# VectorE turns the normalized y of all chunks, and B with x, in a fused Mamba-2 and LoRA layer

## What is computed

```python
x = x + attn(xn) + ffn(xn)                     # xn = layernorm(x), [1, 2048, 1024]
# attn, a Mamba-2 mixer: 64 heads of 64, 8 groups, state size 128
proj = xn @ in_proj_w.T                        # gate 4096 | x 4096, B 1024, C 1024 | dt 64
xBC  = silu(causal_conv4(proj[x|B|C]) + conv_bias)
dt   = softplus(dt + dt_bias);  dA = exp(-dt * exp(A_log))
state = state * dA_t + (dt_t * x_t) B_t        # scan over the tokens, per head
y_t  = state C_t + D * x_t
yn   = y * rsqrt(mean(y*y over the group's 512) + eps) * norm_w * silu(gate)
attn = yn @ out_proj_w.T
# ffn: xn @ W_base.T + b_base, plus the top-2 of 8 rank-16 LoRA experts
```

## Time and profile before

| | |
|---|---|
| median of 3 runs | 3144.74 us (3143.58 to 3145.55) |
| profiled execution, own time | 3145.09 us |
| its span, first to last instruction | 3143.4 us |
| PE, PEld busy | 3126.1 us (99%), 2573.4 us (82%) |
| DVE, ACT, POOL busy | 2558.5 (81%), 1704.5 (54%), 835.5 us (27%) |
| granted clock of TensorE, mean | 1.000 |

### The profile page before, as it was taken

One profiled execution on the slowest core, in us unless ns is written; L12 is line 12 of the kernel. 1 busy time (PEld: TensorE's weight loads), 2 busy tenths in 40 slices (PEclk: granted clock), 3 DMA queues, 4 the chain that ended last, 5 costly groups with the idle time before them and its releaser, 6 DMA issues.

```text
span 3143.4 us, 55218 instructions
## 1 busy us (share of the span) xinstructions
PE 3126.1 (99%) x17660; PEld 2573.4 (82%) x17660; DVE 2558.5 (81%) x4599; ACT 1704.5 (54%) x4467; POOL 835.5 (27%) x917
## 2 busy tenths in 40 slices
PE   8999999999999999999999999999999999999999
PEld 7788888887888888888788888888878888888887
DVE  7977777785589999999648999999954988989983
ACT  5766666664265555656226555556533655565551
POOL 4444434433022222222103222222210222222220
PEclk9999999999999999999999999999999999999999
DMA  8777777777665555555566555555546555555554
GB/s 290 274 265 272 264 276 266 261 256 263 232 216 194 189 201 187 189 194 201 173 225 205 191 191 191 201 184 190 209 166 236 196 195 187 195 194 201 186 189 161
DMA packets 185668, 672.63 MB, mean 214 GB/s; under 512 B 21056, under 2 KB 22208, under 8 KB 185408
## 3 DMA queue, kind: packets, MB, share of 16 engines
q1 hardware_dynamic: 161280, 584.91, 53.3%
q10 hardware_dynamic: 24128, 84.42, 7.6%
HBM read 532.41 MB, written 136.84 MB: 213 GB/s over the span
## 4 chain that ended last, share of the span: by engine, by line
PE 95%; DVE 2%; ACT 1%; DMA 1%; issue 0%; SPq 0%; POOL 0%; ACTq 0%; DVEq 0%; POOLq 0%
PE dense L1072 21%; PE dense L1074 21%; PE dense L1073 21%; PE pX L1072 7%; PE pX L1074 7%; PE pX L1073 6%; PE pY L1187 3%; PE pD L1217 1%; PE pD L1187 1%; DVE conv_us L1497 1%; PE pCB L1163 1%; PE pU L1072 1%; PE pS L1073 1%; PE pS L1072 1%; PE pS L1074 1%; PE pU L1074 1%
## 5 line engine op out<-in xcount | busy, mean ns | idle before, releaser
L1072 PE MATMUL dense<-xn_hi,w_hl 128*128 128x512 f32 (+2 forms) x2192 | 869.7, 397 | 0.8 <-POOL w_hl L444 0.5
L1074 PE MATMUL dense<-xn_hi,w_hl 128*128 128x512 f32 (+2 forms) x2192 | 853.7, 389 | 0.0
L1073 PE MATMUL dense<-xn_lo,w_hl 128*128 128x512 f32 (+2 forms) x2192 | 852.0, 389 | 0.0
L1497 DVE SCALAR_TENSOR_TENSOR conv_us<-conv_in,const_g,conv_us 128x512 f32<-128x512 f32 x576 | 480.3, 834 | 47.0 <-ACT conv_us L694 33.2
L1074 PEld LDWEIGHTS dense<-xn_hi,w_hl 128*128 128x128 f32 (+1 forms) x2192 | 409.5, 187 | 88.9
L1072 PEld LDWEIGHTS dense<-xn_hi,w_hl 128*128 128x128 f32 (+1 forms) x2192 | 409.9, 187 | 86.0 <-issue 2.2
L1073 PEld LDWEIGHTS dense<-xn_lo,w_hl 128*128 128x128 f32 (+1 forms) x2192 | 410.3, 187 | 83.5 <-issue 1.2
L1072 PE MATMUL dense<-z_hi,w_hl 128*128 128x512 f32 x820 | 324.4, 396 | 1.6 <-DVE acc L1680 1.1
L501 POOL TENSOR_TENSOR C_lo<-BC,C_hi 128x128 fp32r<-128x128 f32 x120 | 60.0, 500 | 983.5 <-ACT S_hi L736 982.9
L1074 PE MATMUL dense<-z_hi,w_hl 128*128 128x512 f32 x820 | 319.7, 390 | 0.0
L1073 PE MATMUL dense<-z_lo,w_hl 128*128 128x512 f32 x820 | 319.1, 389 | 0.0
(11 more groups left out here) (233 smaller groups left out, 5935.3 us busy)
## 6 DMA issues: line engine op xcount, KB each, us to landing
w_hl<-w_split SPq DMA_DIRECT2D x732, 512.0 KB, 3.5
w_split<-w_hl SPq DMA_DIRECT2D x244, 512.0 KB, 3.8
cum_b<-cum_scratch ACTq DMA_DIRECT2D x128, 512.0 KB, 4.9
w_raw<-w_slots_dram SPq DMA_DIRECT2D x122, 512.0 KB, 5.4
acc<-x_tr_dram ACTq DMA_DIRECT2D x16, 512.0 KB, 6.5
out_tr_dram<-acc ACTq DMA_DIRECT2D x16, 512.0 KB, 4.7
BC<-x_tok_dram SPq DMA_DIRECT2D x6, 512.0 KB, 5.3
conv_us<-x_tok_dram SPq DMA_DIRECT2D x6, 512.0 KB, 6.2
```

Source lines behind the costliest of these rows:

```text
L1072: nc.tensor.matmul(out, lhs[0], rhs[0], start=start, stop=False)
L1073: nc.tensor.matmul(out, lhs[0], rhs[1], start=False, stop=False)
L1074: return nc.tensor.matmul(out, lhs[1], rhs[0], start=False, stop=stop)
L1497: nc.vector.scalar_tensor_tensor(out=conv_u[r], in0=conv_in[r][:, t:t + TB], scalar=const_g[p][:, 4 * j + t:4 * j + t + 1], in1=conv_u[r], ...
```

## The change

x, B and C of a group become one tensor xBC of six tiles; xT and BC are views of it. `x_rows` turns five tiles instead of four, so B of two chunks comes with x of two chunks, and `B_rows`, B_tm and its semaphore go. In paired groups `chunk_3` goes; yn_rows, gated_pair, z_high_pair and gated_lo_pair take the first chunk of a pair as an argument and are used for chunks 0 and 1 and for chunks 2 and 3. Only chunk 3 of group 0 is still turned by PE in group 1. `chunk_1_x` and `chunk_1_cb` of paired groups are split into `wx_product`, `dtx_product`, `b_low` and `cb_masked`, and ACT's `chunk_1` into `b_high`, `cs_high`, `ramps`, `wx_high`. The lists of DVE and ACT in paired groups are ordered anew, and PE's chunk_1 of chunks 0 and 1 each move behind one more unit. Block 0 and the groups 0 keep their order.

```diff
+        xBC = [sb(f"xBC{i}", [128, XT + 2, TB]) for i in range(2)]
+        xT = [t[:, 0:XT, :] for t in xBC]
+        BC = [t[:, XT:XT + 2, :] for t in xBC]
...
-        x_tm = sb("x_tm", [128, 2, GC])
-        B_tm = sb("B_tm", [128, NC, N])
+        x_tm = sb("x_tm", [128, 2, GC + N])
```

ScalarE's list of a paired group:

```diff
                     gate_unit(0)
-                    normalize(g - 1, 3, second)
+                    if second:
+                        z_high_pair(g - 1, 1 - p, 2)
+                    else:
+                        normalize(0, 3)
+                    cs_high(g, p, 0)
                     gate_unit(1)
-                    chunk_1(g, p, 0, last, two=True)
-                    z_high(g - 1, 3)
+                    b_high(g, 0, True)
+                    wx_high(g, 0)
+                    if not second:
+                        z_high(0, 3)
                     skip(g, 0)
                     gate_unit(2)
                     gate_unit(3)
+                    b_high(g, 1, True)
+                    ramps(g, 0, True)
+                    next_cum(g, 0, last)
                     skip(g, 1)
-                    chunk_1(g, p, 1, last, two=True)
+                    wx_high(g, 1)
+                    cs_high(g, p, 1)
+                    ramps(g, 1, True)
+                    next_cum(g, 1, last)
...
                     skip(g, 3)
-                    z_high_pair(g, p)
+                    z_high_pair(g, p, 0)
                     if not last:
                         x_unit(2)
-                        x_unit(3)
-                        x_unit(4)
                     mean_square(g, 2, True)
                     mean_square(g, 3, True)
+                    if not last:
+                        x_unit(3)
+                    normalize(g, 2, True)
+                    normalize(g, 3, True)
                     if last:
-                        normalize(7, 2, True)
-                        normalize(7, 3, True)
-                        z_high(7, 2)
-                        z_high(7, 3)
-                    else:
-                        normalize(g, 2, True)
+                        z_high_pair(7, 1, 2)
+                    else:
+                        x_unit(4)
                         x_unit(5)
-                        z_high(g, 2)
                         tanh_conv(g, 5)
```

TensorE's list, and the transposes of VectorE:

```diff
                     gate_unit(g, False, 0, True)
-                    if second:
-                        chunk_3(g - 1, 2, two=True)
                     gate_unit(g, False, 1, True)
+                    gate_unit(g, False, 2, True)
+                    if not second:
+                        chunk_3(0, 3)
                     chunk_1(g, 0, p, True, True)
-                    gate_unit(g, False, 2, True)
-                    chunk_3(g - 1, 3, two=second)
                     gate_unit(g, False, 3, True)
                     chunk_2s(g, 0)
                     chunk_2b(g, 0)
                     out_units(g, 0, two=True)
+                    out_units(g, 1, two=True)
                     chunk_1(g, 1, p, True, True)
-                    out_units(g, 1, two=True)
...
-                    x_units(2)
-                    if last:
-                        chunk_3(7, 2, two=True)
-                        x_units(1)
-                        chunk_3(7, 3, two=True)
-                        x_units(1)
+                    x_units(4 if last else 2)
...
                         for k in range(4):
-                            src = xT[p][32 * f:32 * f + 32, :, :].rearrange("n j (c t) -> n j c t", c=NC)
-                            dst = x_tm[32 * k:32 * k + 32, :, :].rearrange("p c (j i) -> p j c i", j=XT)
+                            src = xBC[p][32 * f:32 * f + 32, 0:XT + 1, :].rearrange("n j (c t) -> n j c t", c=NC)
+                            dst = x_tm[32 * k:32 * k + 32, :, :].rearrange("p c (j i) -> p j c i", j=XT + 1)
```

VectorE's list of a paired group:

```diff
-                    x_rows(g, 0, p, 1 if second else 0, 4)
-                    chunk_1_x(g, 0, True)
-                    gated(g - 1, 3)
-                    chunk_1_cb(g, 0, True)
-                    gated_lo(g - 1, 3)
+                    x_rows(g, 0, p, 0, 1)
+                    if second:
+                        silu(g - 1, 5, p)
+                        prep(g)
+                    x_rows(g, 0, p, 1, 4)
+                    wx_product(g, 0)
+                    if second:
+                        gated_lo_pair(g - 1, 1 - p, 2)
+                        b_low(g, 0)
+                    else:
+                        gated(0, 3)
+                        b_low(g, 0)
+                        gated_lo(0, 3)
                     gate_tile(g, 0, False)
                     gate_tile(g, 1, False)
-                    masked(g, 0, True)
+                    cb_masked(g, 0)
+                    dtx_product(g, 0)
+                    y_state(g, 0, True)
+                    y_skip(g, 0, True)
+                    state(g, 0)
                     gate_tile(g, 2, False)
+                    gate_tile(g, 3, False)
...
+                    wx_product(g, 1)
+                    dtx_product(g, 1)
+                    b_low(g, 1)
                     dve.wait_ge(acc_loaded, (q + 1) * 64)
-                    chunk_1_x(g, 1, True)
                     out_adds(g, 0, halves=(0,), two=True)
+                    masked(g, 0, True)
...
-                    chunk_1_x(g, 2, True)
-                    chunk_1_cb(g, 2, True)
+                    wx_product(g, 2)
+                    b_low(g, 2)
+                    dtx_product(g, 2)
+                    cb_masked(g, 2)
...
-                    x_unit(j_first + 2)
-                    x_unit(j_first + 3)
...
-                    x_unit(j_first + 4)
-                    if not last:
-                        x_rows(g + 1, 0, 1 - p, 0, 1)
-                    x_unit(j_first + 5)
-                    if not last:
-                        B_rows(g + 1, 1 - p, 0, 2)
-                    gated(g, 2)
-                    gated_lo(g, 2)
...
-                        silu(g, 5, 1 - p)
-                        B_rows(g + 1, 1 - p, 2, 4)
-                        prep(g + 1)
+                        y_state(g, 3, True)
+                        y_skip(g, 3, True)
+                        state(g, 3)
+                        y_intra(g, 2, True)
+                        y_intra(g, 3, True)
+                        x_unit(2)
+                        x_unit(3)
+                        yn_rows(g, p, 2, 0, 1)
+                        conv_tap(g, 4, p, 0)
+                        yn_rows(g, p, 2, 1, 2)
+                        conv_tap(g, 4, p, 1)
+                        yn_rows(g, p, 2, 2, 3)
+                        conv_tap(g, 4, p, 2)
+                        yn_rows(g, p, 2, 3, 4)
+                        silu(g, 3, 1 - p)
+                        gated_pair(g, p, 2)
+                        conv_taps(g, 5, p)
+                        silu(g, 4, 1 - p)
```

More of the change, by code:

```diff
@@ L721, in wx_high, with cs_high @@
+                def cs_high(g, p, c):
+                    if first_block and c == 0:
+                        return
+                    if c == 0:
+                        act.wait_ge(post, post_n(q, g, NSET - 1))
+                    nc.scalar.activation(C_hi[:], CT[p][:, c * Q:(c + 1) * Q], ACT.Copy)
+                    act.wait_ge(s_upd, grp(q, g) * S_STEPS + (c + 2 if c else 1))
+                    nc.scalar.activation(S_hi[:], state_at(g, c), ACT.Copy).then_inc(cs_hi, 1)
                 def wx_high(g, c):
-                    act.wait_ge(xw_done, chunk(q, g, c) * 2 + 2)
+                    if last_block and c == NC - 1:
+                        return
+                    act.wait_ge(xw_done, chunk(q, g, c) * 2 + (1 if g > 0 and not first_block else 2))
@@ L723, in wx_high, with ramps @@
                     nc.scalar.activation(wx_hi[:], wx[:], ACT.Copy).then_inc(wx_hi_done, 1)
-                def chunk_1(g, p, c, last=False, behind_exp=None, two=False, behind_wx=None):
+                def ramps(g, c, two=False):
                     n, E_c = chunk(q, g, c), E_2[half_of(two, c)]
                     E_flat = E_c.rearrange("p h t -> p (h t)")
[L728 to L741, removed]
@@ L753, in chunk_1, with next_cum @@
                                              scale=-1.0).then_inc(exp_done, 1)
[L754 to L759, removed]
+                def next_cum(g, c, last):
                     if c < 2:
@@ L764, in chunk_1 @@
                         load_cum(g + 1, c - 2)
+                def chunk_1(g, p, c, last=False, behind_exp=None):
+                    b_high(g, c)
+                    cs_high(g, p, c)
+                    ramps(g, c)
+                    if behind_exp is not None:
+                        behind_exp()
+                    wx_high(g, c)
+                    if c >= 1:
+                        normalize(g, c - 1)
+                    next_cum(g, c, last)
                 def skip(g, c):
@@ L968, in paired_group @@
                     mean_square(g, 1, True)
[L969 to L973, removed]
```

(18 more changed lines are left out.)

194 lines of the change are left out of this document (111 added, 83 removed).

## The result

| kernel | median us (runs) | ratio to before, 95% interval |
|---|---|---|
| before | 3144.16 (3143.48 to 3145.55) | 1 |
| after | 3206.49 (3205.03 to 3208.12) | 1.0198 (1.018 to 1.0215) |

The change makes the kernel 2.0% slower, 62 us; 3188 was forecast, 18 us too little. The profiled execution has a span of 3205.8 us.

The account below looks back on a forecast made before the run. PE, 99% busy, was the bound; DVE's loop of 91.2 us would replace it. +15.2 us each in blocks 1 and 2 and +13.1 in block 3, +43.5 on 3145.1, gave 3188 us; forecast 3174 to 3205, range 3152 to 3213.

Parts of the forecast that it names:

- PE loses 20.2 us: PE in groups 1 to 7 of three blocks: 42 chunk_3 of 0.48 us go; its loop falls from 88.08 to 87.12.
- DVE's and ACT's loop becomes 91.2: One paired group on DVE with its waits for ACT: from 87.45 to 91.2 us, in block 3 90.1.
- Stretch A: DVE's list from the end of masked(3) to the first gate tile: 35.97 us before, 37.95 forecast.
- Stretch C: DVE's list from y_intra(0) to the end of masked(3): 30.15 us, same work in the same order.
- stretch B: DVE's list from the gate tiles to y_intra(0): 21.96 us before, 23.19 forecast.
- From the start of the block to group 2: +0.1: First group's y_intra to chunk_2b of group 2: the new loops need what the old did, +0.1 us.
- PE stops where it needs B_lo: At chunk_2b: PE stops 4.1 us per group, about 1 us of it earlier, at gate unit 2 and chunk_1(0).
- PE pays for its stops: Rival: PE runs slowly after each stop, losing 1.7 us per stop, mostly hidden; with no room 3215 us; chance 0.11.
- DVE's loop stays below 87.12: Rival, paired groups: PE stays the bound and all 20.2 us come in, 3125 us; 3120 to 3139 has chance 0.07.
- half the surplus: Rival: 1.2 to 2.5 us of DVE's waits and lengthenings vanish, loop 88.7 to 90, time 3152 to 3172; chance 0.12.
- round trips: DVE's five waits for ACT per group, 5.1 us in all, said to stay when DVE is late as a whole.
- Transposes belong on PE: Rival, advice against the change: 0.12 us per tile on PE against 0.89 on DVE; no other time, no own chance.

Follow-up runs that it names:

- v2_lists: v1_lists with the last half of yn_rows of chunks 0 and 1 behind state(2) and ACT's chunk 3 work ahead of tile 1; nothing left out: 3128.74 us, 0.9951.
- e1_filler: Changed kernel plus ten overwritten 512-column matmuls per group where PE stands before chunk 0's B_lo, in groups 2 to 6 and group 1: 3211.87 us, 1.0216 of before.
- e2_yn12: Changed kernel without 4 of 16 stream transposes of chunks 2 and 3 in groups 1 to 6 of blocks 1 to 3 (y partly stale): 3173.31 us, 1.009.
- v1_lists: Changed kernel, all transposes kept on DVE, with DVE's and ACT's lists reordered so that DVE's waits are filled; nothing left out: 3139.47 us, 0.9984 of before.
- e4_pe_back: Changed kernel's new lists and fifth tile, but PE again turns y of chunks 2 and 3 of groups 1 to 6: 3140.96 us, 0.9988 of before.

## Why the prediction came out as it did

The mechanism was the forecast's, and the size 30% short: 44 us slower were forecast, and 62 measured. The distances from prep to prep give the whole 62 us: five loops of 91.93 against 88.08 are +19.3 in block 1, +20.4 in block 2 (one of its loops took 93.07), and +16.8 in block 3; the start of a block up to prep of group 2 +2.3 in each; group 7 and what follows -1.0 in blocks 1 and 2, nothing in block 3; block 0 +1.1.

**PE loses 20.2 us.** Right: 168 instructions, and v2_lists shows PE's loop in block 3 at the forecast's length.

**DVE's and ACT's loop becomes 91.2.** Right in kind, 0.7 short. Stretch A was to be 37.95 and is 37.88 (end of masked(3) to the gate tiles, 1096.36 to 1134.24). Within it x_rows cost 0.51 each as said, yn_rows 0.44, the new wait before the taps of tile 5 was 0.42 for 0.5, and B_lo beside GpSimd 1.28 from start to next start, less the usual 0.20: 1.1 for 1.2. Stretch C, forecast at 30.15, is 30.08. The miss is stretch B: 1134.24 to 1158.21 are 23.97, and 23.19 were forecast. The copy of const_g now meets GpSimd and takes 0.52 instead of 0.18; what the rest is was not taken apart. Changes between transposes and other instructions, at up to 0.1 each, are a part of it; I had counted none for the order new in B. In block 3 the loop is 90.75 for 90.1. These 0.65 to 0.73 over fifteen loops are 10.5 us, the larger part of the miss; the loop of 93.07, with its 13 slow matmuls, is 1.1 more. Block 0, which was to stay, is 1.1 longer, and group 7 gives 0.8 more than forecast.

**From the start of the block to group 2: +0.1.** This step failed. I let DVE come forward by 1.4 us only, and supposed that the old length would hold. Measured are 5.1 less from prep of group 0 up to prep of group 1 (69.46 for 74.53) and 7.4 more up to that of group 2 (96.9 for 89.5), +2.3 in sum. I had expected that DVE would run until it waits for PE and that the old length follows from there. It does wait for PE, the last time at 952.62, for 2.27 us of pS (in block 1; e1_filler's matmuls, put in just there, come out at prep of group 2 for that reason). Behind that it waits for ACT alone, and its own list, with the sixteen transposes in it, decides: the stretch is 95.44 in e2_yn12 with four transposes less, and 93.33 in v1_lists, with nothing done to PE. Three blocks make 6.6 us.

**PE stops where it needs B_lo.** Right: 18 stops of 2.3 to 3.1 us at that matmul. The 4.1 us that were to be the stop are 4.8 now, of which PE stands for 3.1 and loses 1.6 in the slow matmuls, or, where the clock stays up, stands a second time for 0.9. A stop of 1 us at gate unit 2 was forecast and is not there.

**PE pays for its stops.** This rival had the right place and, at ten of 18 stops, a right price (1.7 us per stop forecast, 1.6 measured). e1_filler and the six loops without slow matmuls show that it costs nothing as a rule: the time falls into the slack that DVE's longer loop leaves. Only the loop of 93.07 pays, 1.1 us. I had explained it by the first transposes of the run, with the clock at 1.00. Here it is the granted clock that drops, which is another cause; that its price came out about the same is luck.

**The rivals with a shorter loop.** "DVE's loop stays below 87.12" and "half the surplus" did not come for this order, but v1_lists shows that waits of the kind they counted on can be filled: 3.65 us per loop came back, and with v2_lists' order the time is 3129, near the 3125 to 3132 that the first of them gives. The prediction called the round trips fixed ("the wait stays when DVE is late as a whole"). That holds against lateness: from gated_pair to z_lo 11.84 us pass in v1_lists as well. It does not hold against order, since DVE's own work can stand in the wait.

**Ports and transposes.** The lengthening of B_lo, and of taps and silu in v2_lists, follows GpSimd's work beside them. By SBUF — State Buffer, section "SBUF: two separate sides", of the Trainium skill, GpSimd, when it reads SBUF, and a VectorE instruction with two SBUF inputs shut each other out of a shared pair of ports for a whole instruction. The 1.35 us of B_lo, which end 0.14 after GpSimd's, and the 3.32, 1.53 and 1.38 that shrink in v2_lists when transposes take their place, agree. "Transposes belong on PE" held at this order, 3206 against 3141 in e4_pe_back; where DVE's waits are filled it does not decide, since v2_lists with all of them on DVE is 0.4% faster than e4_pe_back.

## What to carry to other kernels

Before work is moved, work out the loop of each engine by itself, with its waits on round trips: here the receiver's loop grew by 4.5 us (from 87.45, as the prediction reads it, to 91.93) with 0.6 to spare, and the kernel's loop by 3.9, whatever the giver saved. Such a wait is room for the receiver's own work, and in this kernel GpSimd's work in SBUF does less harm beside VectorE's transposes: with the same sixteen transposes one order is 62 us slower than before, and another 16 us faster. Whether a hole of TensorE and the slow matmuls behind it cost time is told by filling the hole, or by a loop of the same trace that has no slow matmuls.

## What the runs showed of the hardware

- After a stop of TensorE of 2.9 us in a stream that had been gapless, the granted clock was 0.79, 0.50 and 0.82 in the three windows up to 1140, and eight matmuls of 512 columns took 3.3 us (most 0.43 from start to start) instead of 1.8. This happened around ten of 18 stops of 2.3 to 3.1 us; what parts them from the other eight stays open. With the hole filled up to 0.83 us the clock stayed at 1.00 (e1_filler).
- Stream transposes of VectorE were not lengthened beside GpSimd (0.45 us each beside S_lo and C_lo in v2_lists), while beside it taps with all inputs in SBUF took 1.0 us more for three, and a 128x128 subtraction 1.1 us more (changed kernel).
- A stream transpose of 32x320 takes 0.51 us, one of 32x256 0.44: the fifth tile costs 0.07 and not a quarter of 0.44.
